# Third sublayer's attention: VectorE takes the masked minima ahead of the attended rows' remainder and of the scaling of the next probabilities

## The reference

```python
def _L1_xattn_ref(q, k, v, mask, Wq, Wk, Wv, Wo, bo):   # HEADS = 16, DIM_HEAD = 64
    qh = heads_split(q @ Wq)
    kh = heads_split(k @ Wk)
    vh = heads_split(v @ Wv)
    dots = jnp.einsum('bhid,bhjd->bhij', qh, kh) * scale
    dots = jnp.where(mask[:, None, :, :], -jnp.finfo(dots.dtype).max, dots)
    attn = jax.nn.softmax(dots, axis=-1)
    out = jnp.einsum('bhij,bhjd->bhid', attn, vh)
    return out.transpose(0, 2, 1, 3).reshape(b, n, h * d) @ Wo + bo
...
x = x + _L1_xattn_ref(_layernorm(x, axis=-1), ctx_1024, ctx_1024, mask_BxSxS2_bk1, ...)
```

## Time and profile before

| what | value |
|---|---|
| median of 3 runs | 1508.84 us |
| the profiled execution's own time | 1509.0 us |
| its span in the profile | 1507.3 us |
| mean granted TensorE clock | 0.984 |
| busy TensorE matmul / VectorE / ScalarE / GpSimd | 93% / 68% / 52% / 20% |
| the attention of the third sublayer, first scores to the last projection | about 513 us to 1022 us |

### The profile page before, as it was taken

How to read it: one execution, slowest core, us unless ns; L and a number is a source line. 1 busy time by engine, 2 the same in 40 slices (tenths; PEclk the granted TensorE clock), 3 DMA queues, 4 the chain that set the end, 5 groups by cost and what they waited for, 6 DMA issues and landing times.

```text
span 1507.3 us, 27410 instructions
## 1 busy us (share of the span) xinstructions
PE 1408.2 (93%) x9946; PEld 1125.7 (75%) x9946; DVE 1020.9 (68%) x2452; ACT 779.4 (52%) x1674; POOL 294.1 (20%) x331
## 2 busy tenths in 40 slices
PE   6899999998999788999999999988999999999998
PEld 5899987884556556666666666666889999999997
DVE  6767772655567678876767777785577766767753
ACT  4556663345676466677677777763353222222221
POOL 0000001251452504100000000022223323323321
PEclk9999999998999999999999999999999999999999
DMA  9423103123563101100101000001016555654341
GB/s 348 144 92 101 59 1 117 52 102 136 162 209 114 59 18 29 48 2 1 33 5 30 2 29 2 2 2 34 29 34 157 136 101 119 120 130 115 96 101 56
DMA packets 78479, 117.80 MB, mean 78 GB/s; under 512 B 7487, under 2 KB 51845, under 8 KB 77829
## 3 DMA queue, kind: packets, MB, share of 16 engines
q1 hardware_dynamic: 75269, 107.59, 25.5%
q0 software_dynamic: 3072, 8.39, 1.8%
HBM read 97.09 MB, written 18.87 MB: 77 GB/s over the span
## 4 chain that ended last, share of the span: by engine, by line
PE 51%; DVE 8%; ACT 4%; issue 4%; DVEq 0%; POOL 0%; ACTq 0%
PE PS L67 12%; PE PS L68 12%; PE PS L69 12%; PE PS L2561 5%; PE PS L2588 4%; PE PS L2603 3%; PE PS L2575 3%; ACT c_pr L2675 3%; DVE c_sm L2791 2%; DVE c_pr L2800 1%; DVE c_u L2804 1%; ACT c_pt L2684 1%; PE PS L1891 0%; DVE c_rl L2796 0%; DVE c_c L2764 0%
## 5 line engine op out<-in xcount | busy, mean ns | idle before, releaser
L1964 ACT ACTIVATE d_hf<-PS,C 128x512 f32<-128x512 f32 x160 | 108.8, 689 | 267.7 <-PE PS L69 263.8
L2684 ACT ACTIVATE c_pt<-PS 100x512 f32<-100x512 f32 x256 | 138.7, 594 | 113.0 <-PE PS L2575 111.0
L949 POOL CAST d_h<-d_hf 128x512 fp32r<-128x512 f32 x160 | 127.9, 812 | 307.5 <-DVE d_hf L2046 251.7
L67 PE MATMUL PS<-d_w,d_h 128*128 128x256 f32 x640 | 183.3, 286 | 2.6 <-issue 1.4
L68 PE MATMUL PS<-d_w,d_h 128*128 128x256 f32 x640 | 181.0, 283 | 0.0
L69 PE MATMUL PS<-d_w,d_h 128*128 128x256 f32 x640 | 181.0, 283 | 0.0
L2675 ACT ACTIVATE c_pr<-c_sm,c_mn 128x400 f32<-128x400 f32 x256 | 158.7, 625 | 32.6 <-DVE c_mn L2791 32.6
L2791 DVE CUSTOM_DVE_ANT_0 c_sm<-PS,c_mw 128x400 f32<-128x400 f32 x256 | 136.0, 569 | 32.9 <-PE PS L2561 27.8
L2561 PEld LDWEIGHTS PS<-c_k,c_q 64*128 64x128 f32 x768 | 62.3, 187 | 113.0 <-DVE c_mn L2791 70.5
L2561 PE MATMUL PS<-c_k,c_q 64*128 64x400 f32 x768 | 105.5, 380 | 40.5 <-DVE c_mn L2791 39.1
L954 DVE TENSOR_TENSOR d_h<-d_hf,d_h 128x512 fp32r<-128x512 f32 x160 | 131.8, 881 | 13.1 <-POOL d_h L949 13.1
(11 more groups left out here) (304 smaller groups left out, 3186.0 us busy)
## 6 DMA issues: line engine op xcount, KB each, us to landing
d_wb<-wscratch SPq DMA_DIRECT2D x64, 512.0 KB, 7.6
a_cT<-ctxT SPq DMA_DIRECT2D x4, 1601.0 KB, 8.4
a_raw_nat<-ctx SPq DMA_DIRECT2D x4, 1536.0 KB
zs<-e_zero SPq DMA_DIRECT2D x2, 2944.0 KB, 22.0
ys<-e_y SPq DMA_DIRECT2D x46, 128.0 KB, 1.8
d_w1r<-l_w SPq DMA_DIRECT2D x10, 512.0 KB, 4.0
d_w2r<-l_w SPq DMA_DIRECT2D x10, 512.0 KB, 5.1
e_z<-zs SPq DMA_DIRECT2D x9, 512.0 KB, 4.2
```

Source lines behind the costliest of these rows:

```text
L67: pe.matmul(out, w[0], x[0], start=first, stop=False)
L949: i = eng.tensor_copy(mem["h"][b % 2][0][:, m, :], mem["hf"][:, m, :])
L1964: act.activation(memD["hf"][:, m, :], PS[:, m, :], ACT.Silu, bias=C[:, b1 + g * 4 + m:b1 + g * 4 + m + 1]).then_inc(DM["act"], 1)
L2684: act.activation(c_pt[u % 2][0:KW, :, :, i * P + r * DH:i * P + (r + 1) * DH].rearrange("p h t q -> p (h t) q"), PS[0:KW, BT + r, :].rearr ...
```

## The change

In VectorE's list, the two steps `masked(s + 2)` and `attended(u - 1)` go to the head of each tile's part, ahead of `normalised(s + 1)` and `low_queries(u + 1)`. Nothing is added or removed, and the other engines' lists and every wait stay as they are.

```diff
             for u in range(UNITS + 2):
                 for i in range(QT):
                     s = u * QT + i
+                    if s + 2 < UNITS * QT:
+                        masked(s + 2)
+                    if i == 3 and 1 <= u <= UNITS:
+                        attended(u - 1)
                     if s + 1 < UNITS * QT:
                         normalised(s + 1)
                     if i == 1 and 1 <= u < UNITS - 1:
                         low_queries(u + 1)
-                    if i == 3 and 1 <= u <= UNITS:
-                        attended(u - 1)
-                    if s + 2 < UNITS * QT:
-                        masked(s + 2)
                     if i == 0:
                         if u + 1 < UNITS:
                             low_keys(u + 1)
```

## The result

The changed kernel takes 1596.85 us (1592.92 to 1602.31, 4 runs) against 1509.28 us of the kernel before (4 runs): a ratio of 1.057, with a 95% interval from 1.0543 to 1.0597. It is **87.6 us slower**. The sign was forecast; the forecast size was 44.6 us, and the time lies outside the range of 1536 to 1575 us. The profiled execution took 1599.8 us, with a span of 1598.1 us and a mean granted TensorE clock of 0.959, where the one before had 1509.0 us, 1507.3 us and 0.984.

A forecast was written before the change was run, and what follows sets the result against it. TensorE was taken to bound the kernel. Costs of 68.4 us (second tile) and 3 us (transposes), less a 26.8 us credit (fourth tile), gave +44.6 us, 1553.4 us; range of eight in ten 1536 to 1575.

The forecast's parts named there:

- What bounds: Whole kernel: TensorE bounds, 93% busy, so reordering VectorE acts only by making gaps on TensorE shorter or longer.
- the second tile: Queries' low part falls behind minima and scaling, so the attended product starts 2.28 us later in 30 units: 68.4 us.
- The fourth tile's credit: Minima start earlier there, so the next scores' waits of 37.0 us in all shrink: 26.8 us gained.
- The 3 us for the transposes: Fourth tile, six context units: the second head's transposes wait 0.5 us each for the later scaling, 3 us lost.
- "Zero" for the first tile: First tile: no TensorE step waits for the minima or scaling there, so neither gain nor cost.
- one kind of gap only: TensorE's gaps before: only scores waiting for minima to free their banks, 35 waits, 37.0 us.
- An undisturbed unit: Sign: from the first tile's scores to the next unit's should take 16.5 us, where it took 14.88.
- The bank rule: Second tile: exposed read-out of the shared bank priced at 0.69 us, 21 us in all; 2.28 us was preferred.
- rival 4: More slow: transposes wait in every unit, +71 us, 1580; or clock at 0.95, +25, 1578. Above 1572: 10%.
- The faster one: Rival: first tile's gap goes and the second tile doesn't pay; -26.8 us, down to -37.0, about 1482 us; chance 4%.

The follow-up runs named there:

- Experiment 1: Changed kernel with the old order (scaling, queries' low part, minima) back in the second tile alone; 1487.27 us, ratio 0.9845 to the kernel before.
- experiment 2: Kernel before with the new order (minima, scaling, queries' low part) in the second tile alone; 1619.26 us, ratio 1.0717.
- Experiment 11: Experiment 1's kernel with the keys' low part also moved ahead of the scaling in the first tile; 1476.11 us, ratio 0.9759 to the kernel before.
- experiment 7: Changed kernel with scaling, minima, queries' low part in the second tile; 1563.80 us on a slower chip, ratio 1.0117 to the kernel before.
- experiment 5: Changed kernel with six useless matmuls ahead of the attended product's first half; 1592.82 us on a slower chip, ratio 1.0297 to the kernel before.

## Why the prediction was wrong

- **What bounds, and the second tile: right.** The debit was 30 gaps of 2.28 us, 68.4; measured 30 gaps, 70.4 us, 2.29 in the undisturbed unit. The second tile's scores are followed by the third's after 5.43 us (847.16 to 852.59), where 5.3 was forecast. Experiment 1 takes exactly this away and experiment 2 does it alone.
- **The fourth tile's credit: right in kind.** 26.8 us were credited, the scores' waits fell by 31.8. The 3 us for the transposes came out as 2.9. The scores of the first tile follow those of the fourth after 858.11 - 855.64 = 2.47 us, where it was 870.50 - 867.33 = 3.17.
- **"Zero" for the first tile: too low.** From its scores to the second tile's it takes 864.03 - 858.11 = 5.92 us against 5.60. Part is a longer transposing run, for the scaling is only just in time, and part the values waiting for the keys' low part (1.9 us more in all). It was passed over as "no TensorE step waits", and as one kind of gap only, though TensorE already waited 2.9 us for the keys' low part. An undisturbed unit takes 858.11 - 841.26 = 16.85 us, where 16.5 was forecast. Summed over the 32 units, the way from the first tile's scores to the second's, less half of its time at half clock, grows from 175.1 to 187.7 us; 4.8 of these 12.6 us are in the waits above, and the rest covers the 6.3 us left over. Experiment 11, which puts the keys' low part ahead of the scaling, goes from the ratio 0.9845 of experiment 1 to 0.9759, though by the estimate 7.6 us of these 13 are clock (23.8 us lost there, 16.2 here), most of it ahead of 540 us, where the edit changes nothing.
- **The bank rule.** The Trainium skill's "Perfetto Trace Analysis", section Matmuls, read as a price would have made 21 us of the debit; the runs agree with the 2.28 us of the order, and with the same bank but the old order the wait is 1.1 us (experiment 1). Separate banks were not tried.
- **The step that failed is the clock, in rival 4.** It says of the gap at 825.83 in a stretch of clock 1.00: "So gaps of this length alone did not lower it", and puts the worst case at a clock of 0.95, +25 us, outside the sum. What the runs show in its place: a gap of 2.3 us is followed by 1.2 GHz more often than not. I counted TensorE's gaps over 2 us in the attention from 540 us, and how many have a stretch at half clock beginning inside them or within 2 us of their end: 3 of 7 before, 19 of 30 with the change, 21 of 30 in its second profile. In experiment 7 none of the attended product's 29 gaps of 1.4 to 1.5 us has one, and of all its 34 gaps between 1.2 and 2 us 1 has. The kernel before already had a rate, 3 of 7, and a price: the three stretches last 3.4, 3.4 and 6.8 us, and half of that is lost. By these, 30 new gaps make 13 falls and 29 us, an estimate that belonged in the sum. Measured were 16 more falls behind such gaps and 41.4 us, since the rate was higher and 9 of the 20 stretches last 6.8 us. One counterexample of a thing that happens behind some gaps and not behind others was taken for a rule; what decides between them was not looked into.
- **The rivals.** The faster one needed the queries' low part to be written by 862.40, and with the second tile's order kept that is what experiment 1 does. Its price, -26.8, came out as -22.5. The Trainium skill's "Perfetto Trace Analysis", section Optimization Strategy, is borne out there: making the step that the gaps wait for start sooner did pay, where it didn't open gaps elsewhere.

The sum with the term that was missing: 44.6 + 41.4 = 86.0 us, against 87.6 measured. That it comes so near is in part luck: the credit was 5.0 us too small, the debit 1.7 us, the values' 1.9 us and the 6.3 left over were missing, and the profiled execution is 3 us above the median.

## What to carry to other kernels

Before a step is moved ahead of others on an in-order engine, ask at each place in the loop whether its inputs are there by then: where they come late, everything that it overtook waits with it. Here a repeated gap of 2.3 us on TensorE was paid twice, once by its length and once by the clock behind it, and a gap of 1.4 us once; count in the kernel at hand how many such gaps are followed by a half-speed stretch, over all of them and not at one. Reorder per place, not per loop: taking the minima first gave 18 us in one tile and cost 109 in another.

## What was not expected of the hardware

- Idle gaps of 2.3 us are followed by TensorE's lower clock in about 6 of 10 cases (19 and 21 of 30), gaps of 1.4 us in none of 29, and useless matmuls in the gap prevent it: 42.3 us gained by adding 180 of them.
- A matmul of fp32 operands, 128 x 128 by 128 columns, was issued as two, at 0.12 us apiece in a row (24 in 2.94 us); one such pair alone took 0.49 us.
- The chips differ: the kernel before took 1509.8 and 1513.0 us on two, and 1546.9 us on a third, where in the run of experiment 5 the attention began at about 543 us in place of 515. The ratios agree: 1.0297 and 1.029 for the same kernel, 0.9741 and 0.9721 for another. Why that chip is slower ahead of the attention was not looked into.
